# Attention over four images: the low part of the probabilities one quad later, and the copy of scores between two exponentials

## What is computed

```
q, k = Wq x + bq, Wk x + bk          # 32 channels
v    = Wv x + bv                     # 256 channels
att  = softmax(q^T k / sqrt(32))     # 4096 x 4096
out  = Wf [ gamma * (v att^T) ; x ] + bf
```

## Time and profile before

| | |
|---|---|
| median of 3 runs | 1958.57 us (1958.51 to 1958.60) |
| the profiled execution: its own time | 1958.0 us |
| the profiled execution: span of its instructions | 1956.1 us |
| busy: PE, PEld, DVE, ACT, POOL | 99%, 97%, 86%, 87%, 72% |
| granted TensorE clock | 1.0 throughout |
| matmuls | 15656 |

### The profile page before, as it was taken

The page is one execution under the profiler, slowest core; times in us unless marked ns, Lnnn a source line. Parts: engine busy times, 40 slices in busy tenths (PEclk is TensorE's granted clock), DMA queues, the critical chain, the costliest instruction groups (busy, mean ns, idle before and its releaser), DMA issues.

```text
span 1956.1 us, 46462 instructions
## 1 busy us (share of the span) xinstructions
PE 1939.0 (99%) x15656; PEld 1906.4 (97%) x15656; DVE 1683.0 (86%) x2709; ACT 1711.4 (87%) x2291; POOL 1403.7 (72%) x677
## 2 busy tenths in 40 slices
PE   9999999999999999999999999999999999999998
PEld 8899999999989999999988999999998999999998
DVE  7888989887888889898688988899868898888995
ACT  7899999997789999999788999999978899999996
POOL 3678777778467787777747777877765777777775
PEclk9999999999999999999999999999999999999999
DMA  4311111110321111111042111111104111111111
GB/s 144 85 22 18 16 21 22 21 20 15 125 73 23 21 18 17 22 21 22 12 133 65 23 22 19 17 18 21 22 12 136 39 23 22 21 18 17 19 22 17
DMA packets 297832, 69.70 MB, mean 36 GB/s; under 512 B 280544, under 2 KB 281312, under 8 KB 297696
## 3 DMA queue, kind: packets, MB, share of 16 engines
q1 hardware_dynamic: 296880, 67.90, 16.0%
q10 hardware_dynamic: 816, 0.13, 0.0%
HBM read 34.41 MB, written 33.55 MB: 35 GB/s over the span
## 4 chain that ended last, share of the span: by engine, by line
PE 91%; DVE 3%; ACT 2%; issue 2%; POOL 1%; DMA 0%; SPq 0%; DVEq 0%; ACTq 0%; POOLq 0%
PE ps_o L441 71%; PE ps_s L433 11%; PE ps_o L300 4%; PE ps_p L300 4%; PE ps_s L317 1%; DVE top L720 1%; ACT raw L547 1%; PE ps_p L341 1%; PE ps_p L334 1%; ACT ps_p L640 1%; DVE lo L766 1%; ACT hi L633 0%; DMA raw<-wf1T 0%; POOL lo L966 0%; POOL raw L935 0%
## 5 line engine op out<-in xcount | busy, mean ns | idle before, releaser
L935 POOL TENSOR_TENSOR raw<-raw,top_m 128x1024 f32<-128x1024 f32 x508 | 1207.9, 2413 | 257.6 <-DVE top_m L755 238.3
L441 PE MATMUL ps_o<-val_hi,hi 128*128 128x258 f32 x4096 | 1002.7, 282 | 3.6 <-ACT hi L633 2.1
L441 PE MATMUL ps_o<-val_lo,hi 128*128 128x256 f32 x4096 | 999.6, 280 | 0.0
L441 PEld LDWEIGHTS ps_o<-val_hi,hi 128*128 128x128 f32 x4096 | 772.1, 189 | 4.6 <-ACT hi L633 2.5
L441 PEld LDWEIGHTS ps_o<-val_lo,hi 128*128 128x128 f32 x4096 | 770.7, 188 | 0.0
L766 DVE TENSOR_TENSOR lo<-ps_p,hi 128x1024 fp32r<-128x1024 f32 x508 | 617.7, 1216 | 153.0 <-ACT ps_p L640 145.7
L720 DVE TENSOR_TENSOR top<-ps_s,top 128x512 f32<-128x512 f32 x960 | 658.6, 686 | 58.5 <-ACT raw L547 10.4
L633 ACT ACTIVATE hi<-raw 128x1024 fp32r<-128x1024 f32 x508 | 539.7, 1062 | 143.4 <-PE ps_o L441 134.7
L441 PE MATMUL ps_o<-val_hi,lo 128*128 128x258 f32 x4096 | 598.0, 283 | 1.6 <-DVE lo L766 1.3
L547 ACT ACTIVATE raw<-ps_s 128x512 f32<-128x512 f32 x1024 | 553.4, 593 | 30.2 <-DVE top L720 6.0
L441 PEld LDWEIGHTS ps_o<-val_hi,lo 128*128 128x128 f32 x4096 | 534.7, 189 | 3.7 <-DVE lo L766 3.7
(11 more groups left out here) (79 smaller groups left out, 1096.4 us busy)
## 6 DMA issues: line engine op xcount, KB each, us to landing
conv_d<-conv_st SPq DMA_DIRECT2D x64, 256.0 KB, 2.1
result<-conv_d SPq DMA_DIRECT2D x512, 32.0 KB, 1.8
out<-result SPq DMA_DIRECT2D x510, 32.0 KB, 1.6
xf<-x SPq DMA_DIRECT2D x31, 512.0 KB, 3.8
xf<-x SPq DMA_DIRECT2D x2, 256.0 KB, 3.3
raw<-wf2T SPq DMA_DIRECT2D x1, 256.0 KB, 4.5
raw<-wv SPq DMA_DIRECT2D x1, 256.0 KB, 4.0
raw<-wf1T SPq DMA_DIRECT2D x1, 256.0 KB, 5.0
```

Of the source, the lines that this page charges most:

```text
L441: last = nc.tensor.matmul(ps_o[:, i, 0:width], p[:, t % 2, jl * I + i * P:jl * I + (i + 1) * P], v[:, j, 0:width], start=opens and jl == 0 ...
L935: nc.gpsimd.tensor_tensor(raw[:, slot], raw[:, slot], top_m[:, r].unsqueeze(1).broadcast_to((P, JQ, I)), ALU.subtract).then_inc(sub_done, 1)
```

## The change

1. TensorE multiplies the low part of a quad one quad later. Slots 1 to 6 are now lead(t), scores(t+12), and the trail of quad t-1 (`trail_both`). Slot 0 is lead(0), scores, lead(1), with no trail at all (in the first block `lead_first` alone). Slot 7 is lead(0) of quad 7, `trail_both(6)`, trail(0) of quad 7, scores, lead(1), trail(1). The number of matmuls is the same.
2. A new semaphore `lead_done` is sent at the end of each lead. `exponential_hi` of quad t+1 waits for the lead of quad t-1 and for `lo` of quad t-1 (the two readers of its `hi` buffer) instead of for the trail of quad t-1.
3. ScalarE's order is now `exponential_hi`, `keep_scores`, `exponential`: the copies of the scores stand between the two exponentials.
4. VectorE's iteration t now splits quad t (`low_part`), where it split quad t+1. As `lo` has two buffers and the trail runs a quad later, the split waits for the trail of quad t-2. `normalise` of half 0 in quad 7 stands behind the split, and the one of half 1 ahead of the next block's first split.

```diff
@@ TensorE, attend
+                def trail_both(t):
+
+                    if first and t == 0:
+                        pe.wait_ge(lo0_half, b + 1)
+                    pe.wait_ge(lo_done, Q + (t + 1))
+                    for jl in range(JQ):
+                        for i in range(IT):
+                            last = values(t, i, val_hi, lo, CV, False, False, (jl,))
+                    last.then_inc(pv_done, 1)
...
                         scores_ahead(t)
                         scores_ahead(t + 1)
                         lead_first()
-                        for two in (range(0, 2), range(2, JQ)):
-                            if two[0]:
-                                pe.wait_ge(lo_done, Q + 1)
-                            else:
-                                pe.wait_ge(lo0_half, b + 1)
-                            for i in range(IT):
-                                last = values(0, i, val_hi, lo, CV, False, False, two)
-                        last.then_inc(pv_done, 1)
                         continue
                     pe.wait_ge(hi_done, Q + (t + 1))
-                    if 0 < t < QUADS - 1:
+                    if t == 0:
+                        lead(t, 0)
+                        scores_ahead(t)
+                        lead(t, 1).then_inc(lead_done, 1)
+                    elif t < QUADS - 1:
...
+                        last.then_inc(lead_done, 1)
                         if not (first and t == 1):
                             scores_ahead(t)
-                        pe.wait_ge(lo_done, Q + (t + 1))
-                        for jl in range(JQ):
-                            for i in range(IT):
-                                last = values(t, i, val_hi, lo, CV, False, False, (jl,))
-                        last.then_inc(pv_done, 1)
-                        continue
-                    lead(t, 0)
-                    if t == 0:
-                        scores_ahead(t)
-                        pe.wait_ge(lo_done, Q + (t + 1))
-                        trail(t, 0)
-                        lead(t, 1)
-                        trail(t, 1)
+                        trail_both(t - 1)
                     else:
+                        lead(t, 0)
+                        trail_both(t - 1)
                         pe.wait_ge(lo_done, Q + (t + 1))
                         trail(t, 0)
                         scores_ahead(t)
-                        lead(t, 1)
+                        lead(t, 1).then_inc(lead_done, 1)
                         trail(t, 1)
@@ ScalarE, attend
                         else:
-                            act.wait_ge(pv_done, Q + t)
+
+                            act.wait_ge(lead_done, Q + t)
+                            act.wait_ge(lo_done, Q + t)
                         act.wait_ge(sub_done, Q + (t + 2))
                         exponential_hi(t + 1, (QUADS * r + t + 1) % SLOTS)
-                        exponential(Q, t + 1, (QUADS * r + t + 1) % SLOTS)
                     elif not last_image:
...
                     if not (isinstance(n, int) and n * QUADS + t + AHEAD >= STEPS):
+
+                        if first and t == 0:
+                            act.wait_ge(p0_half, b + 1)
+                        act.wait_ge(p_done, Q + (t + 1))
                         keep_scores(H, t + AHEAD, (QUADS * r + t) % SLOTS)
+                    if t < QUADS - 1 or not last_block:
+                        exponential(Q, t + 1, (QUADS * r + t + 1) % SLOTS)
@@ VectorE, attend
+                def low_part(t):
+
+                    if not (first and t == 1):
+                        dve.wait_ge(pv_done, Q + (t - 1))
+                    split_p(Q, t)
+
...
                         normalise(B - 1, 1)
+                        low_part(0)
...
+                    if t > 0:
+                        low_part(t)
+                        if t == 4 and not last_block:
+                            reduce_turned(B + 1)
+                            top_across(B + 1)
+                            spread_top(B + 1, (r + 1) % OUTS)
                     if t == QUADS - 1:
                         normalise(B, 0, first)
...
-                    if t < QUADS - 1 or not last_block:
-                        split_p(Q, t + 1)
```

More of the change, by code:

```diff
@@ L148, in attention_conv @@
             sem("sub_done"), sem("hi_done"), sem("p_done"), sem("lo_done"), sem("pv_done"))
-        o_half_ready = sem("o_half_ready")
+        o_half_ready, lead_done = sem("o_half_ready"), sem("lead_done")
         inv_done, o_scaled, o_turned, finished = sem("inv_done"), sem("o_scaled"), sem("o_turned"), sem("finished")
@@ L451, in lead @@
                         values(t, i, val_hi, hi, CV, t == 0, False, (jl,))
-                        values(t, i, val_lo, hi, C_IN, False, False, (jl,))
+                        last = values(t, i, val_lo, hi, C_IN, False, False, (jl,))
+                    return last
                 def trail(t, i):
@@ L470, in lead_first @@
                             values(0, i, val_hi, hi, CV, True, False, two)
-                            values(0, i, val_lo, hi, C_IN, False, False, two)
+                            last = values(0, i, val_lo, hi, C_IN, False, False, two)
+                    last.then_inc(lead_done, 1)
                 for t in range(QUADS):
@@ L496, in attend @@
                                 values(t, i, val_hi, hi, CV, False, False, (jl,))
-                                values(t, i, val_lo, hi, C_IN, False, False, (jl,))
+                                last = values(t, i, val_lo, hi, C_IN, False, False, (jl,))
+                        last.then_inc(lead_done, 1)
                         if not (first and t == 1):
                             scores_ahead(t)
-                        pe.wait_ge(lo_done, Q + (t + 1))
-                        for jl in range(JQ):
-                            for i in range(IT):
-                                last = values(t, i, val_hi, lo, CV, False, False, (jl,))
-                        last.then_inc(pv_done, 1)
-                        continue
-                    lead(t, 0)
-                    if t == 0:
-                        scores_ahead(t)
-                        pe.wait_ge(lo_done, Q + (t + 1))
-                        trail(t, 0)
-                        lead(t, 1)
-                        trail(t, 1)
-                    else:
+                        trail_both(t - 1)
+                    else:
+                        lead(t, 0)
+                        trail_both(t - 1)
                         pe.wait_ge(lo_done, Q + (t + 1))
@@ L907, in attend @@
                             finish_tile(0)
-                    if t < QUADS - 1 or not last_block:
-                        split_p(Q, t + 1)
[L910 to L914, removed]
+                    if t == QUADS - 1 and last_block and not last_image:
+                        dve.wait_ge(pv_done, Q + t)
                         split_x(snap(dve, b * CHUNKS + CHUNKS), 0)
```

## The result

The changed kernel takes 2026.81 us (median of 4 runs, 2026.12 to 2028.48) where the kernel before takes 1958.54 on the same chips: a ratio of 1.0352, 95% interval 1.0340 to 1.0364. It is 3.5% slower. The forecast was 2024. The profiled execution took 2026.14 with a span of 2024.3, 68.2 us over the span before.

The account below looks back on a forecast made before the run. TensorE was taken to run at its own pace without gaps in the middle of images. Middle blocks 54.6, block 14 2.0, first blocks 3.4 and 6.0 sum to 66.0 on 1958.0: 2024 us, range 1991 to 2040.

Parts of the forecast that it names:

- The middle blocks: Blocks 1 to 13 of four images: TensorE waits for quad 7's low part in slot 7, 1.05 us each, 54.6 in all.
- the chain: From slot 3's folds through reduction, splits, exponentials and copies to quad 7's split, ending at 25.25; TensorE 0.95 us late.
- The lower bound: Slot 7 of middle blocks: with DVE's quad 4 at no cost, some 0.55 us a block still lost.
- the absorbed case: Rival: DVE or ACT catch up after quad 4's reduction before slot 7; 0.55 us a block, 1992 us, chance 0.13.
- the lag of quad 4: VectorE's quad 4 with its reduction takes 5.3 us where a slot has 3.34, delaying the chain into slot 7.
- The first blocks: First block of each image: 3.4 us from changed waits plus 6.0 from VectorE's reduction waiting for POOL.
- The port's 6.0: First blocks: `reduce_top` waits for POOL's subtractions; DVE's lag grows about 2 us in images 0 and 3, 1 in others.
- The other term, 3.4: First blocks: later low part and slot 7 wait against waits removed; +0.5 in images 0 and 3, +1.2 in 1 and 2.
- The estimate of 3: First blocks: the reduction's wait for POOL, if the port is free at each instruction's end, costs nearer 3 us than 6.
- Block 14: No copies after quad 3, but quad 4's reduction and shorter slots: about 0.5 us each, 2.0 in four images.
- The port in every block: Rival: `reduce_top` waits for POOL's last subtraction in each middle block, 0.76 us or more; 2064 us, chance 0.08.
- No new wait: Rival: quad 7's split ends by 24.3, middle blocks stay at TensorE's pace; 1954 to 1959 us, chance 0.08.

Follow-up runs that it names:

- experiment 1: Changed kernel with quad 7's first low part at the end of slot 7, next scores ahead of slot 0's lead, normalisation of half 0 behind the fold: 1971.18 us.
- experiment 2: Changed kernel without VectorE's six `top_across` operations in the attention blocks, group maxima spread directly (output not the reference's): 1993.56 us, ratio 1.0183.
- 3: Changed kernel with, for quad 7 alone, ScalarE's exponential ahead of the copies and VectorE's split ahead of the folds: 2007.20 us, ratio 1.0252.
- experiment 4: Changed kernel with only ScalarE's order undone (exponential_hi, exponential, copies), VectorE keeping the new order: 2569.7 us in one run.
- experiment 7: Changed kernel with a one-SBUF-input reduction of quad 4 in each image's first block: 2022.47 us; the same edit in the kernel before: 1957.51 us.
- Experiment 6: Later low part alone, ScalarE's and VectorE's orders as in the kernel before: 1998.94 us; with one fold moved behind the normalisation of half 1: 1973.54 us.

## Why the prediction was right

Point by point, from the starts of PE's blocks in the two traces.

- **The middle blocks.** Forecast 1.05 us each, 54.6 in 52. In image 0, block 1 to the start of block 14 took 447.38 - 99.77 = 347.61 before and 463.52 - 101.87 = 361.65 after, 14.04 in 13 blocks, 1.08 each, 56 in 52. The place, the releaser and every step of the chain stand as worked out. Experiments 1 to 4 each change a link of it or its due time, and the time follows: 1 and 3 within 1 us of the number written down, 2 and 4 within their ranges (4 in a single run).
- **The lower bound and the absorbed case.** The 0.55 us without the lag of quad 4 is borne out by experiment 2, with 0.51 us a block and 1993.6 in all, as far as its cut goes. The lag was not absorbed in the changed kernel.
- **The first blocks** came out near the forecast in part by luck, as two errors cancel. Forecast 3.4 + 6.0 = 9.4. Image 0 took 30.16 from its first high part to the next block's (71.71 to 101.87) instead of 27.52 (72.25 to 99.77), and the four images together 2.64 + 2.16 + 2.81 + 2.60 = 10.2 more. The port's 6.0 was too high: the reduction's time above 0.42 is 5.1 us in all, and experiment 7 takes 4.0 to 4.3 back (its reduction is itself 0.29 longer than 0.42, four times). The lag beyond that of the kernel before grew by 1.3, 1.1, 0 and 1.2 us where the prediction had 2, 1, 1 and 2, although it had the reduction ready only 1.4 earlier. It also reached PE one link sooner than forecast: as late `hi` of quads 6 and 7 (experiment 7), while the wait for `lo` in slot 7 is 1.0 to 1.2 us by the starts, with the port's lag and without it (1.1 to 1.2 in experiment 7). The other term, 3.4, was too low: 5 to 6 us are left for it, above all in image 2, which had no wait at the port and grew by 2.81 where 1.2 was forecast without the port. Which part of that walk was mis-sized is not shown. The Trainium skill (SBUF — State Buffer, Who interferes with whom) has the two-input VectorE instruction and GpSimd's reads exclude each other for a whole instruction in order of issue. The reduction at 85.57 behind the subtraction begun at about 85.4 agrees. The estimate of 3 that I drew from it in the prediction, with the port free at each instruction's end, was too low against 4.0 to 5.1: in images 0 and 3 the next subtraction had begun 0.2 and 0.4 us before the reduction.
- **Block 14** took 25.35 (463.52 to 488.87) instead of 24.84, 0.51, as forecast (2.3 us in four images, 2.0 forecast); block 15 23.02 instead of 22.97. With 56.6 for the middle blocks of all four images and 10.2 for the first ones that is 69.3; outside the blocks the two traces differ by 1.1 the other way, which gives the 68.2 of the spans.
- **The port in every block** did not come: `top_j` took 0.42 at 338.07, 13.57 into the block, and from 0.42 to 0.61 in the 56 blocks behind the first ones, where it had taken up to 0.56 before.
- **No new wait** was out: PE's matmuls that now stand 16 into slot 7 are late in all 60 blocks that make scores ahead or reduce a maximum.

What I did not see: that slot 0's missing low part leaves the normalisation bare. In the changed kernel VectorE reaches it in time, because the wait in slot 7 and its new order leave it free; I had costed it at nothing with "some 0.9 of 1.43 us". Experiment 6 showed how little that cover was: one split and one fold ahead of it cost 0.46 us a block. The other half, which the move in experiment 1 brought close to the next block, cost 0.09 us a block.

What stays open: the size of the first blocks' term without the port, as said above, and how far a quad 4 shorter than that of experiment 2 would help.

## What to carry to other kernels

Where one engine is full without gaps, moving its work later cannot gain in that stretch; it only moves due times, and the price is read at the one consumer whose due time did not move with the rest (here the last quad, whose low part must end in the same slot). Lay the new order out from measured distances and look for the chain that ends there, from the engine's longest burst on. Two in-order queues that feed each other (ScalarE's exponentials and copies, VectorE's splits and folds) have to be reordered together: one alone gave 2143 us, the other's undoing 2570.

## What the runs showed of the hardware that I had not expected

The granted clock of TensorE held at 1.00 through the waits of 1 us a block in the changed kernel, but not through those of experiment 4. Two stretches of it there, by windows:

```profile
325.00:330.00 5.00, 2.46 (x16) 2.05 (x16) 3.29 (x5) 3.55 (x5) 5.00 (x3) 1.00 0.00 0
330.00:335.00 5.00, 3.92 (x20) 3.92 (x21) 2.37 (x4) 2.26 (x4) 4.24 (x2) 0.66 0.00 0
```

The mean granted clock was 1.00 in the first of these stretches, in which PE was busy for 2.46 of 5 us, and 0.66 in the one after it, so a part of the second ran at the lower of the two levels, 1.2 GHz; over the whole of that run it was 0.96. How much of the 2570 us the lower clock cost and how much the loop is not separated here.
